# A decoder layer's expert outputs: adding each token's two rows inside the scatter

## The reference

```python
logits = xf @ router_w.T
probs = jax.nn.sigmoid(logits.astype(jnp.float32))
topw, sel = jax.lax.top_k(probs, TOP_K)          # TOP_K = 2
topw = topw / (topw.sum(-1, keepdims=True) + 1e-20)
...
h = jnp.square(jax.nn.relu(h))
y = jnp.einsum('tew,ewd->ted', h, W2e)
out = jnp.einsum('ted,te->td', y, combine)       # two experts' rows, weighted and summed
...
x = _layernorm(x + _L0_ffn_ref(x, ...), axis=-1)
```

## Time and profile before

| what | value |
|---|---|
| median of 3 runs | 1151.01 us (1149.64 to 1152.8) |
| the profiled execution | 1156.7 us, its span 1155.0 us |
| first instruction of the last block's work | 672 us |
| first expert row scattered | 966.3 us |
| last expert row scattered | 1127.2 us |
| busy: TensorE, VectorE, ScalarE, GpSimd | 89%, 75%, 51%, 25% of the span |

### The profile page before, as it was taken

How to read it: one execution, slowest core, us unless ns; L and a number is a source line. 1 busy time by engine, 2 the same in 40 slices (tenths; PEclk the granted TensorE clock), 3 DMA queues, 4 the chain that set the end, 5 groups by cost and what they waited for, 6 DMA issues and landing times. The chain is left out here.

```text
span 1155.0 us, 17811 instructions
## 1 busy us (share of the span) xinstructions
PE 1025.4 (89%) x6184; PEld 505.4 (44%) x6184; DVE 867.0 (75%) x1770; ACT 590.7 (51%) x819; POOL 285.5 (25%) x268
## 2 busy tenths in 40 slices
PE   7869999999999999899989779989889888889990
PEld 3433333333333333217778622332323226678880
DVE  4989999988898988405789868878778834745554
ACT  1324555656666666784734226655556552423432
POOL 6743212101115210002210056402020122332222
PEclk9979999999999999998999958999989989989995
DMA  5893140053002000001101034302011020242216
GB/s 192 284 303 61 24 88 2 1 111 87 2 1 69 1 1 1 1 1 32 55 29 39 1 103 124 100 15 65 28 51 29 20 61 26 65 138 79 74 56 223
DMA packets 68889, 76.33 MB, mean 66 GB/s; under 512 B 8828, under 2 KB 62972, under 8 KB 68796
## 3 DMA queue, kind: packets, MB, share of 16 engines
q1 hardware_dynamic: 60108, 60.53, 18.7%
q0 software_dynamic: 3408, 9.34, 2.3%
q10 hardware_dynamic: 5280, 5.25, 1.7%
HBM read 45.37 MB, written 29.15 MB: 65 GB/s over the span
## 5 line engine op out<-in xcount | busy, mean ns | idle before, releaser
L611 DVE TENSOR_REDUCE piece_max<-self_banks 128x1 f32<-128x512 f32 (+3 forms) x640 | 348.9, 604 | 40.4 <-PE self_banks L467 27.0
L558 ACT ACTIVATE early<-self_banks 128x1024 f32<-128x1024 f32 (+3 forms) x320 | 273.6, 895 | 162.2 <-PE self_banks L485 160.5
L1919 DVE TENSOR_REDUCE cross_piece_max<-banks 128x1 f32<-128x512 f32 x256 | 164.0, 683 | 36.2 <-PE banks L1720 35.4
L1844 ACT ACTIVATE cross_probs<-banks 128x1024 f32<-128x1024 f32 x128 | 126.5, 1022 | 104.4 <-PE banks L1743 90.8
L495 PE MATMUL self_banks<-early,V 128*17 128x512 f32 (+3 forms) x1280 | 148.0, 534 | 1.8 <-ACT early L558 1.6
L424 POOL TENSOR_SCALAR_AFFINE_SELECT early<-early 128x512 f32<-128x512 f32 x64 | 40.6, 634 | 349.9 <-ACT early L558 349.6
L1720 PE MATMUL banks<-kx_few,stackx 97*128 97x512 bf16 x256 | 98.0, 423 | 18.4 <-DVE cross_piece_max L1919 9.6
L467 PE MATMUL self_banks<-late 96*128 96x512 bf16 (+3 forms) x256 | 82.3, 342 | 2.5 <-DVE piece_max L611 1.7
L1743 PE MATMUL banks<-stackx,kx_few 99*128 99x512 bf16 x256 | 80.8, 400 | 0.7 <-DMA stackx<-cross_shift 0.6
L1720 PEld LDWEIGHTS banks<-kx_few,stackx 97*128 97x128 bf16 x256 | 25.7, 101 | 112.7 <-DVE cross_piece_max L1919 59.0
L1752 PE MATMUL banks<-cross_probs,vx_few 128*17 128x512 f32 x512 | 72.6, 641 | 0.4 <-ACT cross_probs L1844 0.4
(11 more groups left out here) (295 smaller groups left out, 1842.5 us busy)
## 6 DMA issues: line engine op xcount, KB each, us to landing
stackx<-xparts SPq DMA_DIRECT2D x96, 64.0 KB, 2.3
x_sb<-sent SPq DMA_DIRECT2D x39, 129.0 KB, 2.1
qparts<-late SPq DMA_DIRECT2D x8, 384.0 KB, 3.2
kparts<-late SPq DMA_DIRECT2D x8, 384.0 KB, 5.0
late<-kparts SPq DMA_DIRECT2D x2, 1536.0 KB, 16.5
xparts<-xparts_sb SPq DMA_DIRECT2D x8, 384.0 KB, 2.7
o_tok<-in_w SPq DMA_DIRECT2D x4, 768.0 KB, 5.2
o_tok<-in_w SPq DMA_DIRECT2D x6, 512.0 KB, 4.6
```

The lines of the kernel that those rows point to most:

```text
L558: nc.scalar.activation(probs[:, i % 3, 2 * pair:2 * pair + 2, st["off"]:C], ps[:, 2 * pair:2 * pair + 2, st["off"]:C], ACT.Exp, scale=SCAL ...
L611: nc.vector.tensor_reduce(piece_max[:, u % 2, pc["row"], pc["at"]:pc["at"] + 1], slot[:, 0:pc["w"]], AX.X, ALU.max).then_inc(side_read, 1)
L1844: nc.scalar.activation(probs[:, i % 3, 2 * pair:2 * pair + 2], ps[:, 2 * pair:2 * pair + 2], ACT.Exp, scale=SCALE).then_inc(probs_ready, 1)
L1919: nc.vector.tensor_reduce(piece_max[:, u % 2, pc["row"], pc["at"]:pc["at"] + 1], slot[:, 0:pc["w"]], AX.X, ALU.max).then_inc(side_read, 1)
```

## The change

The second half of `ybuf` goes. Both rows of a token now have the same place, and the scatter adds to what stands there (`compute_op=ALU.add`). For that the buffer is first set to zero, by one DMA on SyncE's queue that reads the 128x128 tile `zeros` again and again, 512 bytes at a time, and writes 2048 + 15 x 128 = 3968 rows of 1 KB, 4.06 MB. GpSimd waits before the first scatter until that has landed, and before each later scatter until the one ahead of it has landed. At the end only four chunks are loaded instead of eight, two on SyncE's queue and two on ScalarE's, straight into `x_sb`, and VectorE has no addition to make.

```diff
-        ybuf = nc.dram_tensor("ybuf", [2 * T + SPARE * P, D], F32).ap()
+        ybuf = nc.dram_tensor("ybuf", [T + SPARE * P, D], F32).ap()
...
                         for n in range(2):
                             sp.dma_start(raw_of(n), pieces_w[n][0]).then_inc(w_in[n], 16)
+                        rows_of_y = (T + SPARE * P) // P
+                        sp.dma_start(ybuf.rearrange("(p a) (b d) -> p (a b) d", p=P, d=P),
+                                     zeros[:].rearrange("p (a d) -> p a d", a=1).to_broadcast([P, 2 * rows_of_y, P])).then_inc(y_cleared, 16)
...
-                        for c in range(NC):
-                            sp.dma_start(o_tok[:, TC * c:TC * (c + 1)], ybuf[c * C:(c + 1) * C].rearrange("(q p) d -> p q d", p=P)
+                        for c in range(0, NC, 2):
+                            sp.dma_start(x_sb[:, TC * c:TC * (c + 1)], ybuf[c * C:(c + 1) * C].rearrange("(q p) d -> p q d", p=P)
                                          ).then_inc(s_yb[c], 16)
...
                             pool.wait_ge(y_read, i + 1)
+                            if i:
+                                pool.wait_ge(s_y[(i - 1) % YR], 16 * ((i - 1) // YR + 1))
+                            else:
+                                pool.wait_ge(y_cleared, 16)
                             nc.gpsimd.indirect_dma_start(ybuf[:], bass.IndirectOffsetOnAxis(xin[:, i % XR, D + 1:ROW].bitcast(U32), 0),
-                                                         ys[:, i % YR], None).then_inc(s_y[i % YR], 16)
+                                                         ys[:, i % YR], None, compute_op=ALU.add).then_inc(s_y[i % YR], 16)
...
-                        for c in range(NC):
-                            act.dma_start(second[:, TC * c:TC * (c + 1)], ybuf[T + c * C:T + (c + 1) * C].rearrange("(q p) d -> p q d", p=P)
+                        for c in range(1, NC, 2):
+                            act.dma_start(x_sb[:, TC * c:TC * (c + 1)], ybuf[c * C:(c + 1) * C].rearrange("(q p) d -> p q d", p=P)
                                           ).then_inc(s_yb[c], 16)
...
                         def added(c):
-                            mine = slice(TC * c, TC * (c + 1))
-                            dve.wait_ge(s_yb[c], 32)
-                            link(nc.vector.tensor_tensor(x_sb[:, mine], o_tok[:, mine], second[:, mine], ALU.add))
+                            dve.wait_ge(s_yb[c], 16)
...
-    places = np.concatenate([(k * T + P * np.arange(NT)[None, :] + rows[:, None]) for k in range(2)]
-                            + [2 * T + P * np.arange(SPARE)[None, :] + rows[:, None]], axis=1).astype(np.uint32)
+    places = np.concatenate([P * np.arange(NT)[None, :] + rows[:, None] for k in range(2)]
+                            + [T + P * np.arange(SPARE)[None, :] + rows[:, None]], axis=1).astype(np.uint32)
```

More of the change, by code:

```diff
@@ L1520, in decoder_layer @@
                 pt, pr = pm[:, 0:2], [po, pm[:, 2]]
-                o_done = sem("o_done")
+                o_done, y_cleared = sem("o_done"), sem("y_cleared")
                 s_xin = [sem(f"xin_in{i}") for i in range(XR)]
```

## The result

The changed kernel takes **1189.02 us** in the median of four runs (1187.34 to 1191.26) against 1151.48 (1149.64 to 1152.8, four runs, one more than ahead of the prediction). The ratio is 1.0328, with a 95% interval of 1.0301 to 1.0355: 3.3% slower, 37.5 us. I had forecast 1161.5 and a range up to 1187. The direction held; the size did not, by a factor of more than three.

A forecast was written before the change was run, and what follows sets the result against it. TensorE, busy 89% of the span, was taken to bound the kernel, other engines counting only where it waits. 12.7 + 1.0 + 1.8 - 5.0 = +10.5 us on the 1151.0 median gave 1161.5, range 1153 to 1187.

The forecast's parts named there:

- so scatters keep pace: Tile loop: one scatter at a time has a period of 3.57 us, below the 3.79 average of 28 intervals.
- My first rival: Tile loop: above an extra of 1.15 us the scatter period exceeds 3.72; +29.0 at 1.8, +47.6 at 2.4; chance 0.24.
- The rule on the add: Scatter's DMA: an add costs only its second read, near 0.3 us instead of the 1.0 taken.
- The clear: SyncE's queue before the cross-attention: 16.8 us of zeros delay the first shift from 690.2 to 702.9, +12.7 us (+5.8 to +34.4).
- the run of 512 bytes: Zeroing DMA on SyncE's queue: 7936 pieces, 496 per DMA engine, each taken at 33.9 ns.
- The line through the two packet sizes: Zeroing DMA: cost per piece interpolated between 256-byte packets at 12 ns and 1 KB stores at 77.6 ns, giving 33.9 ns.
- The end: After the last landing: fewer chunks loaded and no addition, so ScalarE finishes at 1147.8 instead of 1152.80, -5.0 us.
- Tile 8: Tile loop near 1017: its scatter lands 1.0 later, delaying an input buffer's load that TensorE waits for, +1.0 us.
- the landing of the last scatter: End of the tile loop: the last two intervals are shorter than 3.57, so it comes at 1131.38 instead of 1129.60, +1.8.
- the stall of the first scores: Start of the cross-attention: sign that TensorE idles and begins the scores near 703 instead of 690.89.
- TensorE waits for input buffers in the tile loop: Tile loop: a sign that, if seen in the profile after, would show the forecast wrong; no size given.

The follow-up runs named there:

- the early clear: The changed kernel with the same zeroing DMA issued on SyncE's queue in the self-attention, behind the load of x at about 272 us: 1177.05 us, ratio 1.0235.

## Why the prediction was wrong

- **The scatter: here it failed.** The step that failed is "so scatters keep pace". I put the extra of an adding scatter at 1.0 us and the wake-up at 0.15, for a period of 3.57 under the tiles' 3.79. The extra was 1.4: 0.6 of it is GpSimd's own time, which I had left at 0.96 us, and 0.8 the DMA. From the landing to the next scatter it was 0.7, where I had taken the 0.14 us of SyncE's queue. Together that is 4.58, and scatters did not keep pace. Of the 1.01 us missed, this gap is 0.55. Of the price the traces show two sides, next to nothing at a period of 3.16 and some 28 tiles times the excess from 4.00 to 4.58, and my error of 1 us led from the one to the other: the addition cost 28.9 us.
- **What the 0.7 us are.** Not the waking itself. Behind one landing the chain goes on like this:

```profile
1033.57 7.54 DMA ybuf<-ys,x_sb
1041.16 0.70 issue
1041.86 4.18 DMA ybuf<-ys,x_sb
```

The landing is at 1041.11, and 0.05 us later the chain is in "issue", time in which GpSimd waited for nothing that the profile shows. What fills it is not shown. The trace before has no scatter that waits for a landing: behind a row of VectorE the last one starts after 0.28 us (1126.90 to 1127.18), and a second scatter straight behind the first after 0.30.
- **The rival that came true.** My first rival, "the scatter becomes the bound", is what happened. With the measured period, 30 x 4.58 - 111.65 = 25.8, my own sum would have been 12.7 + 25.8 + 1.4 - 5.0 = +34.9, 1186. The rival had 0.24 of my chances, and its numbers ended short because I let the extra alone carry it. Its formula gives 25.8 of the 31.1 us behind tile 8; 3.7 more are in one interval of 8.3 us from 1033.57, whose scatter landed only after the 7.54 us above (the list of landings, up to 4.4, leaves it out), while SyncE stored the padding rows (DMA share 1.07 and 1.12 from 1035 to 1039).
- **The rule on the add.** By the Trainium skill (Collectives: The Full Stack, The bandwidth ceiling, on why ReduceScatter is half of AllGather) an add costs only its second read, for which I had 0.3 us. Of the 1.4 us by which the landing came later, 0.8 lie behind GpSimd's own time, so for a scatter of 128 KB the trace does not agree. (With 0.3 in both places my sum would have been 8.3, not the 8.1 that I wrote.)
- **The clear: right mechanism, size off.** +12.7 forecast; the stall is 8.5 (9.13 - 0.59), the kernel with the clear alone +9.4. The mis-sized term is the run of 512 bytes: 11.7 us x 16 / 7936 = 23.6 ns instead of 33.9. Runs of 512 bytes move at 348 GB/s. In the trace before, the load of x, in packets of about 1 KB, moves at 370 and 337 (278 to 280 and 280 to 282 us), and the weight pieces at up to 412. The Trainium skill's statement (DMA: Bandwidth & Descriptors, Specifications), that 512 bytes are enough for the full rate, agrees with this trace in the main. The line through the two packet sizes was wrong because its upper point came from slow stores: 236 GB/s. That the shift waits its turn behind a large DMA was right, and so was that nothing makes it up.
- **The end: right.** -5.0 forecast, 6.1 in the trace, 5.8 by the kernel with the end alone. ScalarE took 8.03 us for its 16 tiles, where I had 8.5.
- **Tile 8 and the landing of the last scatter**, +1.0 and +1.8 forecast: both were drowned in the loop's pace; the last landing alone cost 3.82 - 2.42 = 1.4. For tile 8 I had misread the chain: its 2.10 us at 1017.58 are "another core or an unknown queue". No load was issued on SyncE's queue between 1003.59 and 1019.63, and TensorE was busy until 1018.15, then idle for 0.78 and 1.07 us, both times until VectorE was done. No run shows the wait for a load that the +1.0 stood for.

Of what I had named as signs, the stall of the first scores (at 698.56, forecast near 703) and the end came about. The clear took about 11.7 us at full share instead of 15 to 18, the first shifts landed up to 10.5 us after issue instead of 12 to 16, and the scatters after 3.8 us instead of 3.4. GpSimd waited for landings in 20 tiles by name, and in more by the count of tiles above, where I had expected VectorE in most. "TensorE waits for input buffers in the tile loop" was the sign of being wrong, and it was there: 24.1 us in 17 tiles.

## What to carry to other kernels

Before work is put one after the other, write down the whole period, the issuing engine's own time and its wake-up included, and compare it with the period of the loop around it; if they lie within a third of each other, the forecast is not one number but two. Take the gap behind a wait from a row of the same engine, with the same kind of instruction behind it and the same kind of event ahead of it; where there is none, as here, give it a range. When a wait is put down to an engine, count how many tiles each side has done before you believe it. A large transfer costs whatever small one is queued behind it, at once or one unit later, and on another queue it costs the loads beside it; it cost nothing that the traces show only where the queue had nothing to do. The best form of this change that was run, with the early clear, is still 2.35% slower than the kernel before, and no complete version beat the kernel before.

## What the runs showed of the hardware that I had not expected

- An indirect DMA of 128 rows of 1 KB that adds to DRAM keeps GpSimd 1.55 us instead of 0.96 and lands after 3.8 us instead of 2.4.
- From a landing to the start of an indirect DMA that waits for it on GpSimd 0.7 us pass; to the start of a memset about 0.1, and to that of a DMA on SyncE 0.14. Memsets in between lengthen the gap by less than their own time: four of them, 1.32 us, from 0.7 to 1.6.
- While a DMA of 4.06 MB is under way on SyncE's queue, the issue of two DMAs of 4 KB behind it takes 9.41 us instead of 1.20.
